# Layer kernel on one core: the logarithm of the norm units by an exponential, a symmetric block of the feed-forward form computed once, units of two batches cut anew, and a new order

## The reference

```
logmap0(x) = arctanh(clip(n, EPS, 1 - 1e-5)) * x / n        # n = |x|
expmap0(v) = tanh(n) * v / n
plin(x, w, b) = expmap0(logmap0(x) @ w + b)
xn = layer_norm(logmap0(x)); xm = expmap0(xn * (1 + sc) + sh)   # before attention, and again before ff
ff = plin(plin(xm, w_f1, b_f1), w_f2, b_f2)
```

## Time and profile before

| | us |
|---|---|
| median of three runs | 1231.22 |
| the runs | 1230.20 to 1233.02 |
| the profiled execution, its own time | 1232.33 |
| its span, first to last instruction | 1230.2 |

### The profile page before, as it was taken

One profiled execution on the slowest core, in us unless ns is written; L12 is line 12 of the kernel. 1 busy time (PEld: TensorE's weight loads), 2 busy tenths in 40 slices (PEclk: granted clock), 3 DMA queues, 4 the chain that ended last, 5 costly groups with the idle time before them and its releaser, 6 DMA issues.

```text
span 1230.2 us, 32690 instructions
## 1 busy us (share of the span) xinstructions
PE 1141.0 (93%) x13168; PEld 810.6 (66%) x13168; DVE 867.6 (71%) x3317; ACT 707.5 (58%) x1434; POOL 238.3 (19%) x336
## 2 busy tenths in 40 slices
PE   6778779999999999999999999999999999999986
PEld 3345445676577577766677677766777777777764
DVE  6779878677877896869766785959477985553332
ACT  1659558576577666577655855667465754434321
POOL 2221022023121202131113121131103130210111
PEclk9989889999999999999999999999999999999998
DMA  9500100000010001000000000000001000000000
GB/s 326 160 21 14 35 15 23 3 28 27 27 36 28 16 24 32 23 19 28 24 32 11 23 15 29 18 19 14 3 19 31 16 16 18 20 3 19 20 9 9
DMA packets 27335, 38.56 MB, mean 31 GB/s; under 512 B 3520, under 2 KB 21312, under 8 KB 27184
## 3 DMA queue, kind: packets, MB, share of 16 engines
q1 hardware_dynamic: 25280, 34.29, 8.6%
q10 hardware_dynamic: 1904, 2.20, 0.6%
HBM read 31.79 MB, written 4.29 MB: 29 GB/s over the span
## 4 chain that ended last, share of the span: by engine, by line
PE 71%; DVE 13%; ACT 9%; issue 4%; DMA 1%; POOL 1%; SPq 1%; DVEq 0%; ACTq 0%; POOLq 0%
PE psg L437 44%; PE psq L437 13%; PE pso L437 7%; PE psg L440 6%; ACT PQ L1390 3%; DVE nm L941 2%; DMA X<-in_x 1%; ACT QK L1390 1%; ACT M L1390 1%; DVE JD L954 1%; DVE U L938 1%; DVE hs L941 1%; ACT JA L1401 1%; DVE TU L938 1%; ACT L1390 1%
## 5 line engine op out<-in xcount | busy, mean ns | idle before, releaser
L1390 ACT ACTIVATE PQ<-psq 128x2048 f32<-128x2048 f32 x112 | 210.3, 1877 | 59.2 <-PE psq L437 58.4
L1759 POOL TENSOR_TENSOR R<-R,rhoT 128x256 f32<-128x256 f32 x128 | 92.7, 745 | 370.2 <-ACT R L1390 370.2
L437 PE MATMUL psq<-QK 32*128 32x128 f32 (+5 forms) x3360 | 131.1, 304 | 1.8 <-DMA QK<-in_w 1.8
L437 PE MATMUL psg<-zT,WiT 128*128 128x256 f32 x512 | 124.4, 386 | 2.5 <-DVE R L938 2.4
L437 PE MATMUL psg<-WoT,R 128*128 128x256 f32 x512 | 116.0, 381 | 1.0 <-DVE R L938 1.0
L437 PE MATMUL pso<-PQ,Vg 128*32 128x256 f32 (+2 forms) x2048 | 111.1, 348 | 5.2 <-ACT PQ L1390 4.0
L437 PEld LDWEIGHTS psq<-QK 32*128 32x128 f32 (+2 forms) x3360 | 97.7, 166 | 26.5 <-issue 21.1
L941 DVE TENSOR_REDUCE nm<-psq 128x16 f32<-128x2048 f32 (+1 forms) x48 | 92.7, 1931 | 23.4 <-PE psq L437 23.0
L437 PEld LDWEIGHTS psg<-WoT,R 128*128 128x128 f32 x512 | 95.1, 190 | 16.2 <-issue 2.4
L437 PEld LDWEIGHTS psg<-zT,WiT 128*128 128x128 f32 x512 | 93.6, 192 | 18.0 <-DVE R L938 4.3
L1390 ACT ACTIVATE R<-psg 128x512 f32<-128x512 f32 x64 | 38.1, 596 | 111.1 <-PE psg L437 111.1
(11 more groups left out here) (223 smaller groups left out, 2273.2 us busy)
## 6 DMA issues: line engine op xcount, KB each, us to landing
bcB<-ada_rows SPq DMA_DIRECT2D x16, 384.0 KB, 3.3
bcA<-ada_rows SPq DMA_DIRECT2D x15, 384.0 KB, 3.4
X<-in_x SPq DMA_DIRECT2D x16, 256.0 KB, 2.8
XR<-in_x SPq DMA_DIRECT2D x16, 256.0 KB, 2.8
out<-XR SPq DMA_DIRECT2D x16, 256.0 KB, 2.1
QK<-NMT SPq DMA_DIRECT2D x128, 3.0 KB
WiT<-in_WiT SPq DMA_DIRECT2D x1, 1024.0 KB, 4.9
WoT<-in_WoT SPq DMA_DIRECT2D x1, 1024.0 KB, 7.4
```

The costliest lines, as they stand in the source:

```text
L437: return e.matmul(o, lhsT, rhs, start=start, stop=stop, skip_group_check=True)
L1390: return e.activation(o, i, func, **kw)
L1759: e.tensor_tensor(R4, R4, rhoT[:, :], ALU.mult).then_inc(*pool_moe.mark(b, f"r{f}{j}"))
```

## The change

Four things. (1) `prep`: the logarithm l of q is first guessed from the bits of q as an integer (`l0`), then ACT takes e = exp(l) of the guess, and a short series in (q-e)/(q+e) corrects it. `Ln` is gone, exponential and tanh share one table. The series that is used for small t has one term more and holds up to 0.2 instead of 0.05. The chain has 43 DVE instructions instead of 34. (2) `WG`: the quadratic form is symmetric, so of its lower half block only the upper one is kept, doubled; the second product (c = 1) starts at column 128 and has 384 columns, when the form is made and when it is used. ACT copies WG in four pieces instead of two. (3) The units: [0], [1, 2], [3, 4], second half of [0], then [5, 6] with [1, 2], [7, 8] with [3, 4], and so on to [13, 14] with [9, 10], [15] with [11, 12]; twelve again. (4) New strings in `ORDER` for all engines.

```diff
-        units = [([0], []), ([1, 2], []), ([3], []), ([], [0])]
-        units += [([2 * i, 2 * i + 1], [2 * i - 3, 2 * i - 2]) for i in range(2, nb // 2)]
-        units += [([], [nb - 3, nb - 2]), ([], [nb - 1])]
+        units = [([0], []), ([1, 2], []), ([3, 4], []), ([], [0])]
+        units += [([i, i + 1], [i - 4, i - 3]) for i in range(5, nb - 1, 2)]
+        units += [([nb - 1], [nb - 5, nb - 4]), ([], [nb - 3, nb - 2]), ([], [nb - 1])]
...
-                        last = mm(psq[:, ic, :], v[:, 128 * ic:128 * ic + 128], v, f == 0, f == 7)
+                        last = mm(psq[:, ic, 128 * ic:512], v[:, 128 * ic:128 * ic + 128], v[:, 128 * ic:512], f == 0, f == 7)
...
-                        last = mm(bank[:, :], mT2[:, c, 128 * t:128 * t + 128], WG[:, c, :], c == 0, c == 1)
+                        last = mm(bank[:, 128 * c:512], mT2[:, c, 128 * t:128 * t + 128], WG[:, c, 128 * c:512], c == 0, c == 1)
...
-                yield from chain(s, u, ("t", "tm", "q", "rec", "q2"), tt(t, z, y, ALU.mult), ts(t, t, TMAX, None, ALU.min),
-                      ts(q, t, -1.0, 1.0, ALU.mult, ALU.add), recip(b, q), stt(q, t, 1.0, b, ALU.add, ALU.mult))
+                yield from chain(s, u, ("t", "tm", "q", "rec", "q2", "l0"), tt(t, z, y, ALU.mult), ts(t, t, TMAX, None, ALU.min),
+                      ts(q, t, -1.0, 1.0, ALU.mult, ALU.add), recip(b, q), stt(q, t, 1.0, b, ALU.add, ALU.mult),
+                      ts(p, q.bitcast(I32), math.log(2) / 2 ** 23, 0.0298 - 127 * math.log(2), ALU.mult, ALU.add))
...
-                w.wait_ge(*act_prep.at(u, "ln"))
-                yield from chain(s, u, ("fl", "e0", "e1", "f", "g0", "g1", "g2"), stt(f, p, 0.5, y, ALU.mult, ALU.mult),
+                w.wait_ge(*act_prep.at(u, "ex"))
+                yield from chain(s, u, ("es", "er", "eg", "u1", "u2", "fl", "fy", "e0", "e1", "f", "g0", "g1", "g2"),
+                      tt(q, q, b, ALU.add), recip(q, q), stt(q, q, 2.0, b, ALU.mult, ALU.mult),
+                      stt(b, q, -3.0, q, ALU.add, ALU.mult), stt(b, b, 6.0, q, ALU.add, ALU.mult),
+                      stt(f, b, -1.0 / 3, f, ALU.mult, ALU.add), tt(f, f, y, ALU.mult),
...
-                w.wait_ge(*dve_prep.at(g, "q2"))
-                if g:
-                    w.wait_ge(*dve_prep.at(g - 1, "fl"))
-                act(lp[:, 6, 0:n], lp[:, 5, 0:n], ACT.Ln).then_inc(*act_prep.mark(g, "ln"))
+                w.wait_ge(*dve_prep.at(g, "l0"))
+                act(lp[:, 3, 0:n], lp[:, 6, 0:n], ACT.Exp).then_inc(*act_prep.mark(g, "ex"))
```

More of the change, by code:

```diff
@@ new lines @@
+        "mmoommaaaaNanaFFqqqqaakonokhkhkkqkwowawwopwppwpawpepemeqqmqaNmFmeaaFaaeaehhekenkeekeekeeeeeekookNwwFFwwa",
+        "owpaowppaaawpppeqmeqmeqmqNmaaFnFaepkhhokeopkkkekeeopeaeoeewweaaeeeeewwawqpppwqamwqmqpemNpamnFFahaphokoeq",
+        "keqqkkkoNekwowwawFFweqapwpaanwpemeeameepmeeahmeaaeehoeeekopkpokkokeqekwewwwawqpppweaqwmeqemeeameemaeeaah",
+        "eeeeeneNaFFakhookpeqkkkopkopwwawwewNpFFppweawqmeqqmapnmpmeaaeaheeaeeaeehkeeeeeeookpekkokeokwewwawqqwqppp",
+        "weaqwmeaemeepmeeameeaeeeeeeahNanakhFFookppkkkeqeokowwawwaewNppFFpweamweqmeqmeemqeaaenpaeaepeeeeeepakooeh",
@@ new lines @@
+        "PqPqPqPqPqPqPqPhhhhPsPssPs*P*P*P*PPPPPPPPPPPPsP*sPsPs*P*P*P*P*Pn*Pn*Pn*Pn*Pn*oPnoPnoP*ooPqoPqoPoPoPoPoPq",
+        "oPqoPoPqoPnoPnoPnPqPnqPnqPnqPnqPqPqPqPqPqPhhhhooPPPffqfqffffffffffqfqfqfffffqfnqfnqfnqfnqnqnqnqfqfqfhfff",
+        "PPPPPhPhPhPPPqPPoPoPoPoPoPPoPoPoPqPoPoPoPoPoPqPoPqPoPoqPoPPPPPPPqPqPqPqPqqqqqqoohNNNfNfNhNfhNfhfofofofoF",
+        "fFfFfoFfnFfnFoFnoFnoFnoFfnFfnFfoFfoFfoFfofofofofofggfgqgfgfgfgfgfggggogogggggfgfgqggfgfgffqgfqgfqfofofof",
+        "qpfqfofqfofqfqfqfsfqfofqfoqsoqohhhhpfpfofofsfofmPoPsoPoPoPomPPPPPPPPPPPPPPPPoPoPPPPPmPfPfmPfPfPfPfPfPfPf",
@@ new lines @@
+        "PfPfPfPfPPPfffffNfNfNfNfNfNfNnnnnnnnffFfffFfFFqFqFFFFFFqFqFqFFqqqgqnoqnoqnoqnoqnqgqnohhhhgnogogogogogogo",
+        "gogogogoogqNgNgNgNgNgNgNwgwgwgwgwgwgwwoopwfwffsfsfsfsffffffffffffffffffwffpfpfffPPPPPPPPPPPPPPPmePqePePe",
+        "PePePqePqmePqePePePePemePqmePFePqePqePqePqePqePqePFePFPqPFPqFPqPFhPFFFhhhFFFeFFFnnnnnnnegggggggeggggggeg",
+        "gggNgNgNgNgNgNgNgggeeoooooooowowowowowooFoooFwFwFwFFFFFFwFwpFFFFoosssggffsfffffffffgfgfggggfwNfgNfgNfgNf",
+        "gNfgNfNfpfgpfgfgggggggggfqfgmfqfgffmqqeemqemeeqeqeqeqeqeFqenqenqenqenqeFhhhhepeFenFenFeFneFoeFoeFsFsFsFs",
@@ new lines @@
+        "FoFoFooogogoooooogogogogeggggggggggeggggggggggooeffwfwfefwfwfwfffffffffffffffffffffffePePwPwPwPPPPPwPwPP",
+        "qPPPPPPPPPPpPpPPPPPPPPPqPPPPPPqPmPwPPPqmqNNpNmNqNnqNnqNnqmqnsqnsqnsqFqnsqhFFFFFFhhhFFFFFFFoFooogggggqoog",
+        "ogogogogoegqeoegeoqqNeoNeoNeoNeoNegNegNegegegegegegegegegegeeegwgwoowwwwwfwfFffffFfFwfFwfqfFfFfFfFFFqfFq",
+        "fpfqfpfqfFqfFqfFfqwfqfFqnqfhfnfnfnfnfgmengngmegpmegggsgssmegsgggghhhggggggggogoggggeeoooooooooooooooooff",
+        "qfffffffffffffwfwffefefwfewfewfewfewewefefwfwfqfefePePeqPpPepPePePePePePePePePePPPPqPPPPPPwPPPPmPqPPPPPP",
@@ L1418, in late @@
                 s = act_late
-                for ic in range(2):
-                    yield
-                    w.wait_ge(*pe_late.at(0, f"W{ic}"))
-                    copy(WG[:, ic, :], psq[:, ic, :]).then_inc(*s.mark(0, f"W{ic}"))
+                yield
+                w.wait_ge(*pe_late.at(0, "W0"))
+                copy(WG[:, 0, 0:128], psq[:, 0, 0:128]).then_inc(*s.mark(0, "W0a"))
+                act(WG[:, 0, 128:256], psq[:, 0, 128:256], ACT.Copy, scale=2.0).then_inc(*s.mark(0, "W0b"))
+                copy(WG[:, 0, 256:512], psq[:, 0, 256:512]).then_inc(*s.mark(0, "W0"))
+                yield
+                w.wait_ge(*pe_late.at(0, "W1"))
+                copy(WG[:, 1, 128:512], psq[:, 1, 128:512]).then_inc(*s.mark(0, "W1"))
                 yield
```

103 lines of the change are left out of this document (43 added, 60 removed).

## The result

The changed kernel takes 1202.3 us (median of four runs, 1200.0 to 1204.9) against 1231.6; the ratio is 0.976 [0.974, 0.978] (here and below the 95% interval stands in brackets). In a later series of five runs it took 1198.2, ratio 0.972 [0.971, 0.974].

The account below looks back on a forecast made before the run. PE's work bounds the middle, chains over ACT, DVE and POOL the first 200 us. 6.5 + 2.6 + 5.3 + 2.0 - 2.5 = 13.9 us less: 1218.4 profiled, 1217.3 as median; range 1207 to 1228.

Parts of the forecast that it names:

- The middle is full: 600 to 700 us, PE busy 98.97 of 100, stands for the whole middle; there the time is PE's work.
- The ff form: 32 products with c = 1 lose 128 columns each, 0.204 us apiece: 6.5 us less, between 6 and 7.8.
- The opening: Up to the first exponential: earlier bias row and no table load, net 2.6 us less, between 1.3 and 3.4.
- The table loads: On ACT, 22 loads become one; four places count, together 5.3 us less, between 3 and 8.
- Nine more instructions: Norm units on DVE: 1.8 us longer each, mostly hidden, so 2.5 us more; ends 0 and 21.6.
- Rival (c): Longer norm units make PE wait in the middle too, 1.8 us each; with all twelve 1236; slower had chance 0.06.
- The exposed place: The norm unit ending at 164.97 us, which PE awaits at 170.19: its added length costs 1.8 us.
- The new order and units: Around the long gap before 170.19 us: net 2 us won, range from 9 won to 3 lost.
- The one gap: PE's 5.88 us standstill until 170.19: batch 4's scores can fill it, but about 4.2 us return as buffer waits.
- (b): The long gap before 170.19 us closes wholly, with its slow clock: 20.9 us less, 1210; chance 0.17.
- M's wait: Sign: PE's wait for the modulated rows of batch 1, 5.88 us before, falls under 4 us.
- the 3.33 us: Sign: PE's idle 3.33 us at the third score step, behind two table loads, is gone.

Follow-up runs that it names:

- L and O: The kernel before with the new logarithm and the new order and units, all 512 columns kept: 1207.7 us, ratio 0.980.
- all three: The changed kernel: symmetric block, new logarithm, new order and units together, against the kernel before: 1202.3 us, ratio 0.976.
- S: The symmetric block (384 columns for c = 1, four copies); alone, in the kernel before with its old order: 1230.1 us, ratio 0.999.
- L alone: The kernel before with only the new logarithm (one table load, nine more DVE instructions per unit), old order and units: 1243.5 us, ratio 1.008.

## Why the forecast was wrong

Step by step, in its own order.

- **The middle is full.** Wrong, and a part of why the order was priced too low. 98.97 of 100 us from 600 to 700 was read as standing for the whole middle. From 200 to 400 us PE was idle for 9.0 us, from 400 to 600 for 4.1; the change took 7.2 of these 13.1. The slices of the page, too, were told wrongly ahead of the forecast: the slices below 9 tenths are the first six, with 6 to 8 tenths, and the last two.
- **The ff form, -6.5 (top 7.8).** The size of the work was right. All products with `WG` take 59.5 us in the trace of L and O and 52.8 in that of all three, the same order with and without S: 6.7 us, 0.21 for each shortened product. Making the form takes 7.47 + 1.46 = 8.9 us instead of 7.03 + 1.88 + 1.88 = 10.8, 1.9 less, which is 8.6 together. PE's work says the same within its scatter: 1112.5 to 1116.8 us in the eight traces without S, 1104.6 to 1109.5 in the nine with it, means 1115.0 and 1106.4. But "PE work removed counts in full" was wrong: in the old order it gave 1 us in the median. In that profiled run, the shortest of twelve, the work fell by 6.3 us and 3.4 came back as idle time, 3.0 of them from 200 to 800 us; where the rest of the median went isn't shown.
- **The opening, -2.6.** Right in place and size: the first exponential starts at 41.22 for a forecast of 41.2. Some of that is luck. The ten products take 7.47 us for the forecast 7.6, but they start 1.43 us later than before, at 28.59, and end at 36.06, not at 34.8 with a wait for U behind them. The later start and the wait that is gone nearly make up for each other.
- **The table loads, -5.3.** Nearly right: one load is left, and taking the loads alone gives 4.9 us in the old order for a forecast of 6.6 with the opening's. Behind 19 of the 22 loads ACT's next instruction starts within 0.02 us, and behind the other three it waits for another engine, so the Trainium skill's drain of 1380 ns (ScalarE: Activation LUTs, "What ACT_TABLE_LOAD costs") is not to be added here.
- **Nine more instructions, +2.5 (ends 0 and 21.6).** In the old order 16 to 18, four fifths of the upper end. Rival (c) came near the sum, but not by its mechanism, a wait of PE for each unit, in the middle too: nothing was added from 200 to 800 us by L alone. The exposed place was read rightly and priced too high, 0.6 us more (5.88 to 6.52) for 1.8. Missed were the opening (PE's wait for U 1.53 to 5.29 us, where the forecast had 0.4), the last batches (3.8 us of idle time from 800 us) and the half clock. In the new order this cost did not come, 4 to 9 us were won instead; nine more steps on top bring it again, 20 to 24 us. That the new order puts other work between a unit and what waits for it is read from the strings and was not measured by itself.
- **The new order and units, +2.0 won (from 9 won to 3 lost).** The step that failed: this term of the sum was far too small. Measured it is 14.3 us won alone and 38 beside the other two. The one gap that it was priced at did close, but the waits of 2.41, 1.92 and 1.98 us that stand for its 5.88 leave 0.7 us of the forecast 2.0. What was won lies at other places, in idle time from 130 to 150 us (4.6 us) and from 200 to 600 (7.2 us), and the forecast put the rest of the strings at nothing. The slow clock behind the gap did go: the ff products there take 3.25 us instead of 5.20. But the time at half clock over the whole kernel stayed, so this was no gain of the sum.
- **The rivals.** (b), 1210, lay nearest. None reached 1202, since each price was taken from the old order's waits, as if the parts could be added. (b)'s own ground, the gap wholly closed with nothing in its place, is not what happened.

Of the signs named beforehand, the one load, the first exponential and M's wait came true, and the 3.33 us shrank to 1.00. PE's busy time fell by 11.0, not 7 to 9. The clock from 150 to 200 us was to be 0.85 or more and was 0.80, with no harm to the time. And "wrong if the middle falls under 97 us in 100" had no force: the kernel before was under it already, with 95.56 and 95.39 from 200 to 400.

What stays open: which of the two, the strings or the units, makes the 14 to 38 us. A kernel with the new units and the old strings, or the other way round, wasn't tried, since the strings call the statistics and the rows of the batches in the order in which their own units need them. Open too is how the interplay of the three parts divides into waits and clock.

## What to carry to other kernels

Read every stretch before calling one "the middle", and sum its idle time: 13 us lay where one good row had closed the case. A wait of 1 us for a chain says that the chain is in time, not that it has room; in a kernel whose order is written out, keep the full length of a longer chain as a price that may well come, and look for where it is late at the ends of the program as well as in the middle. A new order is a term of its own, and its effect doesn't add to the others: the parts alone gave -3 us, together -29, so an edit that looks worthless or harmful in the old order has not been measured until it is run in an order that fits it.
